# An adapter layer's result tile stored in two column pieces instead of one

## What is computed

```python
# layer 0: per-sequence 64x64 mixing, then a gated feed-forward with spline-made weights
x = x + ffn0(mix(x, cond))
# layer 1, first half: a dense product with a low-rank adapter chosen per sequence
H     = einsum('btd,od->bto', x, W)                # 512 -> 512
xa    = einsum('btd,brd->btr', x, A[idx])          # rank 16
z     = H + einsum('btr,bor->bto', xa, Bm[idx]) * s[idx]
# layer 1, second half: a router picks 2 of 8 experts for each token of z
logits = z @ gate_w.T
out    = sum over the token's top 2 of softmax weight * expert(z)
x = x + out
```

## Time and profile before

| | |
|---|---|
| median of 3 runs | 1231.99 us (1231.96 to 1232.45) |
| the profiled execution | 1234.28 us |
| its span, first to last instruction | 1232.5 us |
| mean granted TensorE clock | 0.949 |
| PE busy | 1114.6 us, 90% |
| ACT, DVE, POOL busy | 504.7, 609.3, 740.8 us |
| z stores | 8 DMAs of 1024 KB on queue 10 |
| x1 loads in the layer | 16 DMAs of 512 KB on queue 1 |

### The profile page before, as it was taken

How to read it: one execution, slowest core, us unless ns; L and a number is a source line. 1 busy time by engine, 2 the same in 40 slices (tenths; PEclk the granted TensorE clock), 3 DMA queues, 4 the chain that set the end, 5 groups by cost and what they waited for, 6 DMA issues and landing times. The chain is left out here.

```text
span 1232.5 us, 34938 instructions
## 1 busy us (share of the span) xinstructions
PE 1114.6 (90%) x12488; PEld 1034.1 (84%) x12489; DVE 609.3 (49%) x1161; ACT 504.7 (41%) x994; POOL 740.8 (60%) x1083
## 2 busy tenths in 40 slices
PE   2699999999999998799999459999999999999995
PEld 2689989999989997688998449989898989899994
DVE  9746777767777664335444403333333333333332
ACT  3346777667776665344443112222222222222221
POOL 6668999998999986022433424545455555555553
PEclk9659999999999999689999869999999999999998
DMA  6134554544555543734534513575656565644443
GB/s 260 50 104 154 182 202 159 197 169 152 203 182 174 182 134 142 288 112 142 167 126 144 184 43 69 107 191 144 148 146 148 138 154 130 167 84 71 82 78 58
DMA packets 65921, 177.70 MB, mean 144 GB/s; under 512 B 12656, under 2 KB 21752, under 8 KB 62304
## 3 DMA queue, kind: packets, MB, share of 16 engines
q1 hardware_dynamic: 40736, 127.65, 29.7%
q0 software_dynamic: 19200, 38.94, 17.3%
q10 hardware_dynamic: 5952, 10.65, 2.3%
HBM read 105.84 MB, written 71.38 MB: 144 GB/s over the span
## 5 line engine op out<-in xcount | busy, mean ns | idle before, releaser
L1685 POOL TENSOR_TENSOR idle<-small 128x1 f32<-128x1 f32 x284 | 94.3, 332 | 206.5 <-DMA out<-result,scatter_at 104.3
L958 POOL TENSOR_TENSOR in_lo<-inner,in_hi 128x512 fp32r<-128x512 f32 x128 | 175.5, 1373 | 42.2 <-ACT in_hi L1106 41.9
L1763 PE MATMUL banks<-slots,zt_hi 128*128 x568 | 191.1, 336 | 4.7 <-DVE zt_lo L1852 3.0
L1765 PE MATMUL banks<-slots,zt_lo 128*128 x568 | 184.4, 325 | 0.0
L1764 PE MATMUL banks<-slots,zt_hi 128*128 x568 | 183.6, 323 | 0.0
L1194 DVE TENSOR_TENSOR inner<-silu,banks 128x512 f32<-128x512 f32 x128 | 87.7, 685 | 128.7 <-ACT silu L1101 126.1
L1864 DVE TENSOR_TENSOR hid<-silu_g,banks 128x352 f32<-128x352 f32 x71 | 37.0, 521 | 209.7 <-PE banks L1765 209.7
L1708 POOL DMA_INDIRECT out<-result,scatter_at x71 | 113.6, 1600 | 24.0 <-issue 18.9
L1763 PEld LDWEIGHTS banks<-slots,zt_hi 128*128 128x128 f32 x568 | 107.7, 190 | 7.2 <-issue 6.8
L1830 ACT ACTIVATE zt_hi<-banks 128x512 fp32r<-128x512 f32 x72 | 43.0, 598 | 168.9 <-PE banks L1752 168.9
L1764 PEld LDWEIGHTS banks<-slots,zt_hi 128*128 128x128 f32 x568 | 108.2, 191 | 0.0
(11 more groups left out here) (239 smaller groups left out, 3388.9 us busy)
## 6 DMA issues: line engine op xcount, KB each, us to landing
late_dram<-split_part SPq DMA_DIRECT2D x32, 816.0 KB, 4.3
slots<-late_dram SPq DMA_DIRECT2D x24, 1088.0 KB
raw_part<-in_late_w SPq DMA_DIRECT2D x16, 816.0 KB
x_t<-in_x_t SPq DMA_DIRECT2D x16, 512.0 KB, 3.4
x_both<-in_x_tok SPq DMA_DIRECT2D x16, 512.0 KB, 5.8
x_both<-in_x_res SPq DMA_DIRECT2D x16, 512.0 KB, 3.3
x1t_dram<-x_both SPq DMA_DIRECT2D x16, 512.0 KB, 5.7
x<-x1t_dram SPq DMA_DIRECT2D x16, 512.0 KB
```

Of the source, the lines that this page charges most:

```text
L958: nc.gpsimd.tensor_tensor(in_lo[:, cs, :], inner[u % 2][:, :, :], in_hi[:, cs, :].bitcast(F32), ALU.subtract).then_inc(in_done, 1)
L1685: nc.gpsimd.tensor_tensor(idle[:, at:at + 1], small[:, 0:1], small[:, 0:1], ALU.add)
L1763: nc.tensor.matmul(psum[bank][:, 0:FD], zt_hi[:, k, :], w_high, start=(k == 0), stop=False)
L1765: ins = nc.tensor.matmul(psum[bank][:, 0:FD], zt_lo[:, k, :], w_high, start=False, stop=(k == DK - 1))
```

## The change

The one store at the end of a tile becomes two. Columns 260 to 511 of all four sub-tiles are stored right behind the last half-1 copy, columns 0 to 259 at the end of the tile. Each buffer and piece has its own semaphore. The wait of two tiles later is split in the same way: the second piece's ahead of the first half-1 copy, the other's ahead of the half-0 copies. SP's wait at the end and DVE's ahead of the schedule take both. Each piece has 512 rows, of 1008 and 1040 bytes.

```diff
-        z_stored = [sem(f"z_stored{b}") for b in range(2)]
+        z_stored = [[sem(f"z_stored{b}_{half}") for half in range(2)] for b in range(2)]
...
                 for b in range(2):
-                    sp.wait_ge(z_stored[b], 16 * LNT // 2)
+                    for half in range(2):
+                        sp.wait_ge(z_stored[b][half], 16 * LNT // 2)
...
+                    def store(half):
+
+                        for bank in (Z[0][half], Z[1][half]):
+                            act.wait_ge(drained[bank], use(t, LSUB - 1) + 2)
+                        cols = slice(HALFW, D) if half else slice(0, HALFW)
+                        act.dma_start(z_tiles[bass.ds(t, 1)][:, :, :, cols].rearrange("a p s h -> p (a s) h"), z_out[b][:, :, cols]).then_inc(z_stored[b][half], 16)
+
...
                     if not first:

-                        act.wait_ge(z_stored[b], 16 * n)
+                        act.wait_ge(z_stored[b][1], 16 * n)
                     copy(0, 1)
                     copy(1, 1)
...
                         copy(s, 1)
+                    store(1)
+                    if not first:
+
+                        act.wait_ge(z_stored[b][0], 16 * n)
                     for s in range(LSUB):
                         copy(s, 0)
                         if s == LSUB - 2:
                             shares(t)
-                    for bank in (*Z[0], *Z[1]):
-                        act.wait_ge(drained[bank], use(t, LSUB - 1) + 2)
-                    act.dma_start(z_tiles[bass.ds(t, 1)].rearrange("a p s h -> p (a s) h"), z_out[b][:, :, 0:D]).then_inc(z_stored[b], 16)
+                    store(0)
...
-                dve.wait_ge(z_stored[0], 16 * LNT // 2)
+                dve.wait_ge(z_stored[0][0], 16 * LNT // 2)
+                dve.wait_ge(z_stored[0][1], 16 * LNT // 2)
```

## The result

The changed kernel took 1238.17 us, the median of 6 runs (1236.46 to 1246.96), beside 1231.88 us for the kernel before (6 runs, 1229.96 to 1232.45). The ratio is 1.0055, with a 95% interval of 1.003 to 1.0079: slower by 4 to 10 us, where 1233.6 and no change were forecast.

A forecast was written before the change was run, and what follows sets the result against it. PE was taken to bound the layer, busy 19.9 of 20.5 us in body 4. Terms +1.3 (x1) and +0.3 (block's end) gave +1.6 us, a median of 1233.6 us, range 1230.8 to 1237.0.

The forecast's parts named there:

- ACT's issues: One more DMA issue per tile on ACT, 0.4 us, behind the last half-1 copy, covered by idle time: cost 0.
- rival 4: ACT is held at its issue by SP's, 1.1 us a tile in six tiles: 1240 us, chance 0.05.
- x1: Early piece makes the second x1 load 1.4 us late; PE's next transposes wait, 1.3 us over four bodies.
- Rivals 2 and 3: 2: x1 load delays PE's transposes in every body, 1239 us, chance 0.17; 3: each transfer costs engines its start, 1238.5, 0.03.
- The block's end: Early piece delays body 6's table stores and POOL's chain, 0.3 us; SP's earlier end stays hidden behind POOL, 0.
- The halved rows: Halving the stored rows to about 1 KB loses no DMA rate in the z store: charged nothing.
- The step that failed: Inside the layer PE sets the pace; stores count only where PE or the block's end waits; no removable wait found.
- ACT's part: ACT's added issue, waits on banks, split z waits and the tile-end issue: each charged 0.

The follow-up runs named there:

- e6: The changed kernel again, on chip 5, against the kernel before: 1248.18 us, ratio 1.0046.
- e1: The changed kernel again, on chip 12, against the kernel before: 1219.13 us, ratio 1.0007.
- e8: The changed kernel with POOL's train of eight table stores cut into two groups of four, on chip 5, against the kernel before: 1233.14 us, ratio 0.9927.
- e17: The changed kernel with all 512 columns stored again at the tile's end, on chip 8, against the kernel before: 1250.04 us, ratio 1.0038.
- e2: The changed kernel with both pieces stored at the tile's end, on chip 12, against the kernel before: 1218.94 us, ratio 1.0006.
- e10: The changed kernel with both pieces stored at the tile's end, again on chip 12, against the kernel before: 1221.34 us, ratio 1.0011.
- e14: The changed kernel with both pieces stored at the tile's end, on chip 4, against the kernel before: 1219.13 us, ratio 1.0003.
- e9: The changed kernel once more on chip 12, against the kernel before: 1221.32 us, ratio 1.0006.
- e13: The changed kernel again, on chip 4, against the kernel before: 1219.62 us, ratio 0.9997.
- e7: The kernel before with POOL's eight table stores per tile cut into two groups of four, on chip 5, against the kernel before: 1232.75 us, ratio 0.9922.
- e16: The changed kernel with both pieces stored at the tile's end, on chip 8, against the kernel before: 1246.02 us, ratio 1.0024.
- e11: The changed kernel with all 512 columns stored again at the tile's end, on chip 12, against the kernel before: 1224.03 us, ratio 1.0035.
- e18: The kernel before with table stores in groups of three, three and two, on chip 8, against the kernel before: 1219.07 us, ratio 0.98.

## Why the prediction was wrong

- **ACT's issues: right.** The early piece is issued in 0.4 us, and rival 4 is out. Lines of L1453 in the changed kernel:

```profile
L1453 ACTq DMA_DIRECT2D z_dram<-staging x8: 383/392/410, 534.5 to 678.0; - x8
L1453 ACTq DMA_DIRECT2D z_dram<-x_both x8: 378/383/392, 557.7 to 697.4; - x8
```

- **x1: the step was right, its size too large.** In two of the bodies, 5 and 6, the next transposes waited for it, and PE lost 0.3 us, where 0.2 to 0.5 us in four bodies, 1.3 in all, was forecast. In e6 it was 0.2 us, in e1, with the same loads, nothing. There the room of 0.9 to 1.2 us nearly sufficed; it did not in one body of e8 (2.5 us) and one of e17 (1.7 us), both on chips with holds. Rivals 2 and 3 put the loss at x1 in every body with loads and are out, though their times, 1239 and 1238.5, were the nearest: right in time, wrong in cause.
- **The block's end: right.** POOL is still last. SP's wait ends at 709.4, POOL's drain begins at 710.8, a room of 1.3 us instead of 1.4. So SP's wait did not end earlier for the halved last piece, as was forecast, but nothing hung on it. From body 7 to the experts it took 39.0 us instead of 38.7, which fits the 0.3 us put there:

```profile
L1312 POOLq DRAIN  x1: 5278/5278/5278, 710.8 to 710.8; - x1
```

- **The halved rows: right** as far as shown. Two pieces at the tile's end cost nothing that can be measured on chips 12 and 4 (e2, e10, e14).
- **The step that failed** stands at the very start: "So inside the layer PE sets the pace, and a change of the stores counts only where PE, or the end of the block, comes to wait for something", after which x1 was the only wait inside the layer that was given a price. PE did wait already, for ACT's copies, and ACT for held news of PE. I read body 4, 19.88 us busy of 20.5, as PE's work, while PE needs 19.3 (e1); body 4 was the mildest of six, with a gap of 0.98 us against 2.57 in body 2. I charged ACT's part 0 on the idle time ahead of copies that were released in time, and the two "remote" rows of the list of waits, 15.9 us in 11 waits, I passed over because the profile names no one for them. So the sum lacked a term, the longer holds, which it put at nothing by leaving it out: bodies 1 to 6 took +5.6 us of idle time, 5.1 of it in the gaps of sub-tile 2, and +1.2 us of PE's work at the lower clock, where the sum had +1.3 for x1.
- **What carries this cause.** The change costs nothing that can be told where there are no holds (three runs on two chips, e1, e9, e13), and costs 0.46 to 0.55% on the two chips with holds on which it ran. On one of these, with the train in two, its cost falls from 6.7 us to 0.4. The runs with and without holds show, within their intervals, that the cost needs the holds, and the two pairs of traces say where it falls. The pair e7 and e8 alone carries little, for its intervals leave room for some 5 us and e8 has its wait for x1.
- **What stays open:** why an earlier, split z store makes holds longer. POOL's issues stand at the same places in both kernels. I see one difference: the traffic ahead of the train is over sooner in after, since half the z store is gone from the tile's end, so that the small packets of the table stores flow from 3.3 to 3.7 us into the body instead of 4.4 to 4.6. e16, with both pieces at the end, should have cost nothing if that were all; it cost 0.24% (0.01 to 0.48), which decides neither way. In its profile and that of e17 the packets flow only from 4.2 to 4.7 us on, and the gaps of sub-tile 2 still sum to 18.6 and 19.5 us, so a late start of the packets does not by itself shorten the holds. Nor is it known what in the chip holds the increment, nor whether it is held without the profiler: every execution on record has a profiled span.

## What to carry to other kernels

Before "this engine sets the pace" is believed, compare its busy time in every repetition of the stage, not in one: six equal bodies that last 20.5, 23.2, 21.3, 20.5, 20.5 and 23.1 us are not bound by constant work. Sum the waits whose releaser the profile can't name, and look at what runs meanwhile. Where a long train of GpSimd's indirect DMAs runs beside tightly coupled engines, try it in groups of three with a wait for PE in between, and measure on more than one chip, since the same program took 1219 us on one and 1245 us on another.

## What the hardware showed unexpectedly

- **PE's semaphore increments arrive late beside a train of indirect DMAs.** A finished bank was seen by ACT after 0.11 us (e1), 1.24 us (before), 4.1 us (after), and up to 5.9 us of ACT's time was spent so in one place (e17). The Trainium skill (Perfetto Trace Analysis, section Tensor Engine Instruction) says that a matmul's end in the profile is an estimate and that the update is sent only when PSUM has acknowledged the write, and then has to spread; it gives that no duration. Where nothing is held the traces show no such tail beside the estimated end: in e1 the recorded update stands 0.01 us behind it (median) and ACT's copy 0.11 us. Nothing in that section would give 4 us.
- **The lengths are stepped**: with the train uncut PE's gaps lie at 1.0 to 1.3, 1.8 to 2.8, 3.9 to 4.2 and 5.1 to 5.5 us. The recorded updates of PE show the step itself: held ones follow one another by 1.41 to 1.46 us again and again, a little over the 1.27 us from one table store to the next.
- **Most of the table stores' own updates are missing from the record where there are holds.** 64 stores of 16 increments make 1024; the trace has 286 of them in the changed kernel and 279 in before, but 1023 in e1, e9 and e11. With the train in groups it is 682 (e7), 764 (e8) and 687 (e18). Single updates of ACT and DVE are missing beside the train too, so whether their increments are held as well can't be read.
- **Three in a row did little harm, four did**, each at the one placing tried and on different chips: no "remote" wait in this layer of e18, where ACT waited 2.3 us in all for finished banks, but 22.0 us of "remote" waits in e7. In the bodies that I followed store by store, holds began about the fourth store of a train and ended within 2 us of its last.
- **It depends on the chip**: absent on chips 12 and 4 in every profile, present on 5, 8 and that of the first comparison. Without holds the kernel before takes 1219 to 1221 us, with them 1232 to 1245; on chip 8 the difference is gone in e18 (1219).
- A stall of 3.7 us was followed by 3.2 us of work at the granted clock of 0.50 (599.6 to 602.85), in which half is done, another 1.6 us: body 3 lasts 24.7 us and not 19.3, so this hold was paid for some 1.4 times.
